# Attention masks and a bias spread over both row halves of TensorE, and a new order of blocks in a two-phase software pipeline

## The chip, the cores and the metric

One core of one Trainium2 chip runs the kernel. The metric is device time in microseconds for one launch; lower is better. The kernel before takes 3430.93 us, the median of three runs (3421.76, 3430.93 and 3432.1).

## The reference

Thirty-two independent sequences of 512 rows and 256 columns (`x`, f32) pass through four residual layers, each behind a layer norm:

1. attention A: `x + attn_a(norm(x))`, causal linear attention with 16 heads of 16, feature map `elu + 1`; a running sum of keys times values is carried along the sequence, and numerator is divided by denominator.
2. feed-forward: `x + (relu(norm(x) @ Q(W1).T + b1) @ Q(W2).T + b2)` with 1024 hidden columns; `Q` rounds the weights to -1, 0 or 1.
3. attention B: RMS-normed, rotated queries and keys, 16 query heads on 4 key heads, softmax over a causal window of 64 keys: `mask = (q >= k) & (q - k < 64)`; scores outside of the mask count as minus infinity.
4. the same feed-forward again.

The two things that the change touches in the mathematics are the mask of layer 3 and the bias `b2` of layers 2 and 4. Both are computed as before, in another way.

## The kernel before, in words

Every matrix product is made on TensorE from f32r operands that are split in a high and a low part, so most products are issued as two or three matmuls into the same PSUM bank. There are eight banks: `Q[0..3]` for the attention layers, `HID[0..1]` for the hidden columns and the norms' transposes, `Y[0..1]` for the output of the feed-forward.

**The pipeline.** The main loop runs over sequences; a pass has two phases (`phase1`, `phase2`). In phase 1 sequence `a` is in attention A, in phase 2 sequence `b` (one behind) is in attention B. Beside each attention, TensorE works on feed-forward blocks: `up(fb)` makes 128 of the 1024 hidden columns (four matmuls of 512 columns, L415), `down(fb)` adds them into `Y` (eight of 256 columns, L435). Blocks 0 to 4 (up) and 0 to 3 (down) belong to the turn that starts in this phase ("own"), the rest to the one carried over from the phase before. Between `up` and `down`, ScalarE writes the rectified block (`relu(fb)`, L948 and L949) and VectorE its low part `f_hl` (`low(fb)`, L1305). The first two passes and the last ones are written out; the loop body itself runs 29 times. One call of `phase1` and one of `phase2` make one pass.

**The order of the work is written out by hand**, as a list of block calls for each of TensorE, ScalarE and VectorE in each phase. An engine runs its list strictly in order, and semaphores order the engines among each other. So the place of a block in a list decides what waits behind it.

**Phase 1 blocks.** `qk(j)` and `values` project; `scores(ch, pair)` (L555) is eight matmuls that each use 32 rows of the array; `numer(ch, pair)` (L588, L593) uses tiles of 32 columns; `turn_numer`, `normalise`, `turn_y` (L612), `y_hi` (L1039), `y_lo` (L1437), `project` (L365) and `residual` (L1445) finish a tile of 128 rows. `qkv(t)` projects sequence `b` for phase 2; ScalarE evacuates it as `raw(t)` (L980).

**Phase 2 blocks.** GpSimd squares `raw(t)` (`squares`, L1784), VectorE sums the squares (`sums`, L1537) and makes reciprocal roots (`roots`, L1547 to L1570), then norms and rotates queries and keys (`norm_qk` L1580, `cosines` L1589, `rotate` L1595, with `sines` L1776 and L1777 on GpSimd), and `stack_hi` (ScalarE) and `stack_lo` (VectorE, L1599 and L1601) split them. `turn_qk(t, j)` (L733) transposes them; ScalarE evacuates them (`evacuate`, L1110 for queries, L1113 for keys). `scores(bl)` handles one of eight blocks of 64 queries: first `mask` (L756) writes 0 or -1e30 to two banks `Q[0]` and `Q[1]`, then four score matmuls (L761) add to them, on array rows 0 to 63 for `Q[0]` and 64 to 127 for `Q[1]`; ScalarE takes the exponentials (`exps`, L1122). `numer(bl)` (L822) follows. `own_norm` (L373) transposes the feed-forward's normed input, which `own_apply` (L1291) and `own_norm_lo` (L1297) on VectorE surround.

**The mask before** multiplies the 128-row identity, as stationary operand, with a 128-row mask that is repeated eight times along the 512 moving columns:

```python
pe.matmul(Q[g2][:, :].rearrange("p (u q) -> p u q", u=8), ident_b[:],
          kmask[:, 0 if bl else 1, :].unsqueeze(1).broadcast_to([P, 8, W]), ...)
```

`scores(bl)` issues `mask(bl, 0)` when the exponentials of the block before have left `Q[0]`, and `mask(bl, 1)` when they have left `Q[1]`.

**The bias before.** At the first `down` of a turn both `Y` banks get `b2`, by one matmul each with 64 rows (L431); both use array rows 0 to 63.

The trace takes the branch without `maxima` and `for_max` (`guarded` is false).

Of the kernel before, what the change touches and what calls it, by code (L numbers as in the profile page):

```python
# [26 lines left out]
P = 128  # L27
# [25 lines left out]
_WIDTHS = dict(ident=P, causal=P, heads=HB * HV, parity=2, kodd=W, kfirst=W, qodd=P,  # L53
# [8 lines left out]
def constants():  # L62
# [15 lines left out]
    put("kodd", np.where(odd, 0.0, MASKED))  # L78
    put("kfirst", np.where((k < W) & (k <= qq), 0.0, MASKED))
    put("qodd", np.where(np.tile(odd.T, (2, 1)), 0.0, MASKED))  # L80
    inv = (1.0 / np.float32(10000.0) ** (np.arange(0, HD, 2, dtype=np.float32) / HD)).astype(np.float32)
# [13 lines left out]
def build(nc, x, w_qkv, w_out, w_b, wo_b, gain, mix, w1, b1, w2, b2, const, out):  # L95
    with ExitStack() as ctx:
# [13 lines left out]
        kmask = sb("kmask", [P, 2, W], BF16)  # L110
        qmask = sb("qmask", [P, P], BF16)
        wqkv_h, wqkv_l = (sb(f"wqkv_{n}", [P, KB, 3 * D], F32R) for n in "hl")
# [6 lines left out]
        b2f = sb("b2f", [2 * BR, D])  # L119
        b2r = sb("b2r", [2 * BR, 2, D], F32R)  # L120
        ones_f = sb("ones_f", [P, P])
        share = sb("share", [2 * BR, P], F32R)
# [175 lines left out]
        def _(sp):  # L298
# [13 lines left out]
            sp.dma_start(b2f[:], b2.partition_broadcast(2 * BR)).then_inc(loaded, 16)  # L312
# [41 lines left out]
        def _(pe):  # L354
# [65 lines left out]
            def f_down(turn, fb, tiles=range(NT)):  # L420
# [77 lines left out]
            def program(guarded):  # L498
                def phase1(s):
# [163 lines left out]
                    scores(3, 0)  # L663
                    turn_y(1)
# [3 lines left out]
                    down(1)  # L668
                    up(3)
                    turn_numer(2)  # L670
                    scores(3, 1)
                    numer(3, 0)
                    turn_y(2)
                    next_norm(1)
# [4 lines left out]
                    up(4)  # L679
                    down(2)  # L680
                    turn_y(3)
                    qkv(s.b, 1, a + 1)
                    project(3)
                    qkv(s.b, 2, a + 1)
                    down(3)
                    qkv(s.b, 3, a + 1)

                def phase2(s):
# [182 lines left out]
                    down(7)  # L871
                    numer(0)
                    turn_qk(1, 2)
# [3 lines left out]
                    turn_numer(0)  # L877
                    scores(3)
# [50 lines left out]
        def _(act):  # L929
# [56 lines left out]
            def program(guarded):  # L986
# [91 lines left out]
                def phase2(s):  # L1078
# [63 lines left out]
                    if s.a is not None:  # L1142
                        raw(b, 2)
                        raw(b, 3)
# [700 lines left out]
```

## Time and profile before

| | us |
|---|---|
| median of three runs | 3430.93 |
| profiled execution, its time | 3421.07 |
| profiled execution, its span | 3418.4 |
| mean granted TensorE clock in it | 0.977 of full |

The profiled execution is 9.86 us faster than the median and about equal to the fastest run. Its time is 2.67 us longer than its span.
### The profile page before, as it was taken

How to read it: one execution, taken by the hardware profiler on the slowest of the kernel's cores; microseconds unless marked ns; L12 is line 12 of the kernel's file. 1: busy time of each engine (PE TensorE's matmuls, PEld its weight loads, DVE VectorE, ACT ScalarE, POOL GpSimd, SP SyncE). 2: the span in 40 equal slices, each digit the busy share in tenths (PEclk: the TensorE clock that was granted, in tenths of full speed). 3: DMA queues.
4: the chain of work that ended last, by engine and by line, in shares of the span. 5: the costliest groups of instructions: out<-in, count | busy, mean ns of one | idle time of the engine just before them, and what ended most of it. 6: DMA issues, size and time to landing. Idle time of an engine off the chain costs nothing.

```text
span 3418.4 us, 79649 instructions
## 1 busy us (share of the span) xinstructions
PE 3185.0 (93%) x27330; PEld 2446.4 (72%) x27330; DVE 2384.7 (70%) x5990; ACT 1808.4 (53%) x3585; POOL 532.1 (16%) x1164
## 2 busy tenths in 40 slices
PE   3789999999999999999999999999999999999977
PEld 2567777777777777777777777777777777777755
DVE  5567776776776677777677776677777667777654
ACT  1256555555555556555556545565555556555554
POOL 0011111111111111111111111111111111111111
PEclk9899999999999999999999999999999999999998
DMA  1000000000000000000000000000000000000000
GB/s 58 7 10 16 15 15 2 12 15 15 15 15 2 12 15 15 15 15 2 12 15 15 15 15 2 12 15 15 15 15 2 12 15 15 15 15 2 14 10 15
DMA packets 42021, 44.80 MB, mean 13 GB/s; under 512 B 2609, under 2 KB 41329, under 8 KB 41969
## 3 DMA queue, kind: packets, MB, share of 16 engines
q1 hardware_dynamic: 41968, 44.13, 4.2%
q8 instruction: 29, 0.48, 0.1%
q14 instruction: 24, 0.19, 0.0%
HBM read 21.06 MB, written 16.78 MB: 11 GB/s over the span
## 4 chain that ended last, share of the span: by engine, by line
PE 71%; issue 10%; DVE 9%; POOL 7%; ACT 2%; DVEq 0%; POOLq 0%; SPq 0%; DMA 0%; ACTq 0%
PE Q L365 11%; PE HID L415 11%; PE Y L435 11%; PE Q L555 8%; PE Q L822 4%; PE Q L593 3%; PE Q L588 3%; PE HID L373 3%; PE Q L756 3%; PE Q L761 3%; PE Q L606 2%; DVE f_hl L1305 2%; POOL ff_tmp L1739 2%; PE Q L836 2%; PE HID L733 1%
## 5 line engine op out<-in xcount | busy, mean ns | idle before, releaser
L435 PE MATMUL Y<-w2t,f_hh 128*128 128x256 f32 x2048 | 545.2, 298 | 62.1 <-DVE f_hl L1305 58.8
L435 PE MATMUL Y<-w2t,f_hl 128*128 128x256 f32 x2048 | 516.8, 285 | 0.0
L435 PEld LDWEIGHTS Y<-w2t,f_hh 128*128 128x128 f32 x2048 | 392.9, 192 | 137.0 <-DVE f_hl L1305 92.4
L948 ACT ACTIVATE f_r<-HID,b1c 128x512 f32<-128x512 f32 x512 | 350.5, 684 | 243.4 <-PE HID L415 243.4
L415 PE MATMUL HID<-ff_xh,w1t 128*128 128x512 f32 x1024 | 433.1, 423 | 19.2 <-DVE ff_xl L1297 18.9
L1305 DVE TENSOR_TENSOR f_hl<-f_r,f_hh 128x512 fp32r<-128x512 f32 x512 | 351.6, 687 | 110.6 <-ACT f_hh L949 105.1
L415 PE MATMUL HID<-ff_xl,w1t 128*128 128x512 f32 x1024 | 407.1, 398 | 0.0
L435 PEld LDWEIGHTS Y<-w2t,f_hl 128*128 128x128 f32 x2048 | 394.4, 193 | 5.9
L1407 DVE TENSOR_TENSOR a_s<-Q,cst 128x512 f32<-128x512 f32 x512 | 329.2, 685 | 89.1 <-PE Q L555 84.7
L949 ACT ACTIVATE f_hh<-HID,b1c 128x512 fp32r<-128x512 f32 x512 | 351.4, 686 | 0.0
L1039 ACT ACTIVATE a_yh<-Q 128x256 fp32r<-128x256 f32 x128 | 49.2, 385 | 496.9 <-PE Q L612 496.9
L1122 ACT ACTIVATE a_qz<-Q 128x512 f32<-128x512 f32 x512 | 278.4, 599 | 35.9 <-PE Q L761 34.8
L555 PE MATMUL Q<-a_qz,a_kT 32*128 32x256 f32 x2048 | 290.8, 401 | 2.5 <-DVE a_s L1407 2.5
L415 PEld LDWEIGHTS HID<-ff_xh,w1t 128*128 128x128 f32 x1024 | 194.1, 190 | 89.1 <-DVE ff_xl L1297 34.1
L555 PEld LDWEIGHTS Q<-a_qz,a_kT 32*128 32x128 f32 x2048 | 175.2, 184 | 56.4 <-issue 11.9
L415 PEld LDWEIGHTS HID<-ff_xl,w1t 128*128 128x128 f32 x1024 | 195.3, 191 | 26.4
L756 PE MATMUL Q<-kmask,ident_b 128*128 128x512 bf16 x512 | 166.2, 398 | 40.2 <-ACT a_qz L1122 22.6
L1784 POOL TENSOR_TENSOR a_eq<-a_s 128x320 f32<-128x320 f32 x128 | 97.8, 764 | 654.0 <-ACT a_s L980 616.1
L593 PE MATMUL Q<-a_s,a_v 128*32 128x128 f32 x4096 | 190.2, 275 | 0.5 <-DVE a_state L1417 0.5
L1757 POOL TENSOR_SCALAR at_tmp<-at_mv 128x4 f32<-128x4 f32 x64 | 12.3, 193 | 1100.2 <-DVE at_mv L1283 1100.2
L588 PE MATMUL Q<-a_qT,a_state 128*32 128x128 f32 x3072 | 159.4, 279 | 0.0
L761 PEld LDWEIGHTS Q<-b_qT,b_kT 64*128 64x128 f32 x1024 | 80.1, 194 | 107.4 <-issue 107.4
(185 smaller groups left out, 7079.1 us busy)
## 6 DMA issues: line engine op xcount, KB each, us to landing
x<-in_x SPq DMA_DIRECT2D x32, 512.0 KB, 4.3
out<-x SPq DMA_DIRECT2D x32, 512.0 KB, 3.0
b_vm<-b_v SPq DMA_DIRECT2D x64, 96.0 KB, 2.1
a_s<-in_w SPq DMA_DIRECT2D x1, 1024.0 KB, 8.1
a_qz<-in_w SPq DMA_DIRECT2D x1, 1024.0 KB, 10.5
a_s<-in_w_qkv SPq DMA_DIRECT2D x1, 768.0 KB, 4.6
cst<-in_const SPq DMA_DIRECT2D x1, 389.0 KB, 5.3
a_qT<-in_w_b SPq DMA_DIRECT2D x1, 384.0 KB, 5.8
```

Of the source, the lines that this page charges most:

```text
L365: mm = pe.matmul(dst, a, b, start=(start and k == 0 and j == 0), stop=(last and k == n - 1 and j == 2), skip_group_check=loose)
L415: mm = pe.matmul(HID[fb % 2][:], w1t[:, k, fb * P:(fb + 1) * P], src[:, k, :], start=(k == 0 and j == 0), stop=(k == KB - 1 and j == 1))
L435: mm = pe.matmul(Y[t // 2][:, (t % 2) * D:(t % 2 + 1) * D], h[:, fb % 2, t * P:(t + 1) * P], w2t[:, fb, :], start=False, stop=(fb == FB - ...
L555: mm = pe.matmul(Q[n][:, k * 2 * P:(k + 1) * 2 * P].rearrange("p (e q) -> p e q", e=2), a_kT[rows, k, ch * P:(ch + 1) * P], a_qz[rows, k, ...
L588: pe.matmul(Q[3][VW * j:VW * (j + 1), cols], a_state[:, ch - 1, k, 2 * r + e, :], a_qT[:, k, ch * P:(ch + 1) * P], start=(r == 0), stop=Fa ...
L593: mm = pe.matmul(Q[3][VW * j:VW * (j + 1), cols], a_v[:, ch, k * HB + 2 * r + e, :], a_s[:, ch % 2, r, j * P:(j + 1) * P], start=(ch == 0 ...
L756: pe.matmul(Q[g2][:, :].rearrange("p (u q) -> p u q", u=8), ident_b[:], kmask[:, 0 if bl else 1, :].unsqueeze(1).broadcast_to([P, 8, W]), ...
L948: act.activation(f_r[:, fb % 2, :], HID[fb % 2][:], ACT.Relu, bias=b1c[:, fb:fb + 1]).then_inc(f_rr, 1)
L949: act.activation(f_hh[:, fb % 2, :], HID[fb % 2][:], ACT.Relu, bias=b1c[:, fb:fb + 1]).then_inc(f_act, 1)
L1122: act.activation(b_p[:, bl % 2, g2, :], Q[g2][:, :], ACT.Exp).then_inc(b_ex, 1)
L1305: dve.tensor_tensor(f_hl[:, fb % 2, :], f_r[:, fb % 2, :], f_hh[:, fb % 2, :], ALU.subtract).then_inc(f_lo, 1)
L1407: dve.tensor_tensor(a_s[:, ch % 2, r, :].rearrange("p (h q) -> p h q", h=4), Q[r % 2][:, :].rearrange("p (h q) -> p h q", h=4), causal.uns ...
```

## The change: what it does

Three things, and no instruction of the loop is added or removed.

1. **Mask.** The two mask matmuls of a score block use 64 rows each: rows 0 to 63 for `Q[0]` and rows 64 to 127 for `Q[1]`. The roles are swapped: the transposed mask (`qmask`, which existed for the guarded branch, or the new `qfirst`) is the stationary operand, and a 64-row identity, repeated eight times, moves.
2. **Bias.** `b2r` and `share` get 128 rows; the bias of `Y[0]` uses rows 0 to 63, that of `Y[1]` rows 64 to 127.
3. **Order.** The lists of TensorE, ScalarE and VectorE are rearranged in both phases. Each list holds the same calls as before.

In the set-up, two copies of 64 columns become one of 128, and one subtraction becomes two.

```diff
                     def mask(bl, g2):
-                        pe.matmul(Q[g2][:, :].rearrange("p (u q) -> p u q", u=8), ident_b[:],
-                                  kmask[:, 0 if bl else 1, :].unsqueeze(1).broadcast_to([P, 8, W]),
+                        rows = slice(W * g2, W * g2 + W)
+                        pe.matmul(Q[g2][:, :].rearrange("p (u q) -> p u q", u=8), (qmask if bl else qfirst)[rows, :],
+                                  ident_b[rows, rows].unsqueeze(1).broadcast_to([W, 8, W]),
                                   start=True, stop=False, skip_group_check=True)
...
-                    for y in Y:
-
-                        pe.matmul(y[:], share[:], b2r[:].rearrange("p t n -> p (t n)"), start=True, stop=False,
+                    for j, y in enumerate(Y):
+
+                        rows = slice(2 * BR * j, 2 * BR * j + 2 * BR)
+                        pe.matmul(y[:], share[rows, :], b2r[rows].rearrange("p t n -> p (t n)"), start=True, stop=False,
                                   skip_group_check=True)
```

TensorE, phase 1 (start and end of the list):

```diff
                     up(5)
+                    up(6)
                     values(0)
                     qk(a, 2)
-                    up(6)
                     down(4)
+                    values(1)
                     qk(a, 3)
+                    up(7)
                     down(5)
-                    values(1)
-                    up(7)
+                    down(6)
                     turn_keys(0)
                     turn_keys(1)
-                    down(6)
                     own_norm()
...
                     scores(1, 1)
+                    turn_numer(0)
+                    up(2)
                     numer(1, 0)
-                    turn_numer(0)
                     down(0)
+                    turn_y(0)
                     scores(2, 0)
-                    turn_y(0)
-                    up(2)
                     numer(1, 1)
                     project(0)
                     scores(2, 1)
+                    numer(2, 0)
                     turn_numer(1)
-                    numer(2, 0)
                     scores(3, 0)
+                    down(1)
                     turn_y(1)
                     next_norm(0)
                     numer(2, 1)
                     project(1)
-                    down(1)
...
                     turn_numer(3)
                     up(4)
+                    turn_y(3)
                     down(2)
-                    turn_y(3)
+                    project(3)
                     qkv(s.b, 1, a + 1)
-                    project(3)
                     qkv(s.b, 2, a + 1)
+                    qkv(s.b, 3, a + 1)
                     down(3)
-                    qkv(s.b, 3, a + 1)
```

TensorE, phase 2:

```diff
                     up(5)
+                    up(6)
                     down(4)
-                    up(6)
-                    up(7)
                     down(5)
                     turn_qk(0, 0)
+                    up(7)
                     turn_qk(0, 1)
                     turn_qk(0, 2)
                     scores(0)
+                    down(6)
                     scores(1)
-                    down(6)
                     own_norm()
                     turn_qk(1, 0)
                     turn_qk(1, 1)
                     down(7)
+                    turn_qk(1, 2)
                     numer(0)
-                    turn_qk(1, 2)
                     numer(1)
                     scores(2)
                     up(0)
                     turn_numer(0)
+                    up(1)
                     scores(3)
-                    up(1)
+                    numer(2)
+                    down(0)
                     turn_y(0)
-                    down(0)
                     turn_qk(2, 0)
-                    numer(2)
                     turn_qk(2, 1)
+                    numer(3)
+                    turn_qk(2, 2)
                     project(0)
                     down(1)
-                    turn_qk(2, 2)
-                    numer(3)
                     scores(4)
...
```

Behind these, TensorE's phase 2 changes places of neighbours only. ScalarE's lists change likewise (phase 1: `relu(5)` goes ahead of `qk_exp(1)`, `qk_exp(2)` ahead of `values(0)`; phase 2: `relu(1)` and `exps(3)` go ahead of `y_hi(0)`); its phase 2 up to `exps(2)`, `relu(7)` ahead of `exps(0)` among it, stays. VectorE's ends of phase 1 and its phase 2 where they matter:

```diff
                     residual(2)
                     low(2)
                     normalise(3)
+                    low(3)
+                    y_lo(3)
                     f1_stats(2)
-                    y_lo(3)
-                    low(3)
+                    residual(3)
                     low(4)
-                    residual(3)
                     f1_stats(3)
...
                     norm_qk(2)
                     cosines(2)
-                    rotate(2)
                     norm_qk(3)
                     own_norm_lo()
-                    cosines(3)
-                    rotate(3)
+                    rotate(2)
                     finish_second(s)
...
```

VectorE's phase 2 ahead of `norm_qk(2)` (from `sums(0)` to `low(7)`) is unchanged.

## Rows read from the trace of the kernel before

**Rows 1.** The page, part 1: busy time of each engine over the span

```profile
PE 3185.0 (93%) x27330; PEld 2446.4 (72%) x27330; DVE 2384.7 (70%) x5990; ACT 1808.4 (53%) x3585; POOL 532.1 (16%) x1164
```

**Rows 2.** Stretches: two single passes, then 28 passes; column after POOL: granted clock

```profile
1788.91:1890.55 101.64, 97.77 (x855) 75.24 (x855) 73.67 (x186) 56.35 (x112) 16.61 (x36) 1.00 0.04 12
1992.28:2096.58 104.30, 101.03 (x855) 77.81 (x854) 73.69 (x186) 56.46 (x112) 16.61 (x36) 0.95 0.04 12
303.93:3171.86 2867.93, 2764.30 (x23914) 2128.61 (x23913) 2063.36 (x5209) 1578.57 (x3136) 465.14 (x1008) 0.99 0.04 12
```

**Rows 3.** Waits of TensorE in those 28 passes: total us, times, longest

```profile
PE Y L435 <- DVE f_hl L1305: 47.9, 29, 1.7
PE Q L756 <- ACT a_qz L1122: 19.2, 28, 0.7
PE Q L756 <- ACT b_kT L1113: 13.3, 28, 0.5
PE Q L733 <- ACT b_qT L1110: 8.8, 28, 0.4
PE HID L415 <- DVE ff_xl L1297: 4.0, 19, 0.2
```

**Rows 4.** Timeline of TensorE, end of phase 1 and `turn_qk(1, 0)`: start, duration

```profile
1811.09 0.28 PE L435 MATMUL Y<-w2t,f_hh 128*128 128x256 f32 x1
...
1813.36 0.39 PE L365 MATMUL Q<-wout_h,a_yh 128*128 128x256 f32 x1
...
1814.18 0.34 PE L365 MATMUL Q<-wb_h,at_xh 128*128 128x384 f32 x1
...
1815.23 0.28 PE L435 MATMUL Y<-w2t,f_hh 128*128 128x256 f32 x1
...
1831.34 0.88 PE L733 MATMUL Q<-ident_r,b_qs 128*128 128x128 f32 x8
```

**Rows 5.** Timeline of TensorE: a score block, then a bias and what follows

```profile
1837.35 0.59 PE L756 MATMUL Q<-kmask,ident_b 128*128 128x512 bf16 x2
1837.87 0.50 PE L761 MATMUL Q<-b_qT,b_kT 64*128 64x256 f32 x4
...
1788.91 0.73 PE L431 MATMUL Y<-b2r,share 64*128 64x512 f32 x2
1789.57 0.39 PE L435 MATMUL Y<-w2t,f_hh 128*128 128x256 f32 x1
1789.79 0.28 PE L435 MATMUL Y<-w2t,f_hl 128*128 128x256 f32 x1
1789.91 0.27 PE L435 MATMUL Y<-w2t,f_hh 128*128 128x256 f32 x1
```

**Rows 6.** Timeline of TensorE's weight loads around one score block

```profile
1834.64 0.11 PEld L756 LDWEIGHTS Q<-kmask,ident_b 128*128 128x128 bf16 x2 [0.46 <-issue]
1835.18 0.30 PEld L761 LDWEIGHTS Q<-b_qT,b_kT 64*128 64x128 f32 x4 [0.42 <-issue]
```

**Rows 7.** Timeline of GpSimd and ScalarE, end of phase 1

```profile
1816.50 0.72 POOL L1784 TENSOR_TENSOR a_eq<-a_s 128x320 f32<-128x320 f32 x1 [1.19 <-DVE b_ss L1537]
...
1815.43 0.44 ACT L980 ACTIVATE a_s<-Q 128x320 f32<-128x320 f32 x1 [0.98 <-PE Q L365]
```

**Rows 8.** Timeline of VectorE around that start of phase 2

```profile
1810.86 0.42 DVE L1432 TENSOR_TENSOR a_y<-Q,a_den 128x256 f32<-128x256 f32 x1
...
1815.69 0.18 DVE L1283 BATCH_NORM_AGGREGATE ff_mv<-ff_st 128x2 f32<-128x6 f32 x1 [0.16 <-DVE ff_st L1279]
1821.24 0.92 DVE L1595 TENSOR_TENSOR a_s<-a_s 128x320 f32<-128x320 f32 x1
1822.08 0.68 DVE L1305 TENSOR_TENSOR f_hl<-f_r,f_hh 128x512 fp32r<-128x512 f32 x1
1823.74 0.28 DVE L1601 TENSOR_TENSOR b_ks<-a_s,b_ks 128x128 fp32r<-128x128 f32 x1
1830.99 0.29 DVE L1601 TENSOR_TENSOR b_ks<-a_s,b_ks 128x128 fp32r<-128x128 f32 x1
```

More of the change, by code:

```diff
@@ L893, in phase2 @@
                     turn_y(1)
+                    numer(4)
                     scores(5)
-                    numer(4)
                     project(1)
@@ L900, in phase2 @@
                     next_norm(0)
+                    scores(6)
                     up(3)
+                    next_norm(1)
                     turn_numer(2)
-                    scores(6)
+                    numer(6)
+                    down(2)
                     turn_y(2)
-                    down(2)
-                    next_norm(1)
                     scores(7)
-                    numer(6)
+                    up(4)
                     project(2)
                     numer(7)
-                    up(4)
+                    qk(s.next_a, 0, b)
                     turn_numer(3)
-                    qk(s.next_a, 0, b)
+                    down(3)
                     turn_y(3)
                     qk(s.next_a, 1, b)
-                    down(3)
                     project(3)
@@ L1061, in phase1 @@
                     evacuate_numer(0)
+                    relu(1)
                     y_hi(0)
-                    relu(1)
                     evacuate_numer(1)
@@ L1066, in phase1 @@
                     y_hi(1)
+                    evacuate_numer(2)
                     next_norm(0)
-                    evacuate_numer(2)
                     y_hi(2)
@@ L1143, in phase2 @@
                         raw(b, 2)
+                    if s.a is not None:
                         raw(b, 3)
@@ L1162, in phase2 @@
                     stack_hi(2)
+                    relu(1)
+                    exps(3)
                     y_hi(0)
+                    evacuate(2, 0)
+                    evacuate(2, 1)
+                    evacuate_numer(1)
+                    evacuate(2, 2)
                     stack_hi(3)
-                    relu(1)
-                    evacuate(2, 0)
-                    exps(3)
-                    evacuate(2, 1)
-                    evacuate(2, 2)
-                    evacuate_numer(1)
                     exps(4)
@@ L1179, in phase2 @@
                     next_norm(0)
-                    relu(3)
                     exps(6)
@@ L1184, in phase2 @@
                     exps(7)
+                    relu(3)
                     evacuate_numer(3)
@@ L1213, in _ @@
                 n += 1
-            dve.tensor_tensor(b2r[BR:], b2f[BR:].unsqueeze(1).broadcast_to([BR, 2, D]), b2r[BR:], ALU.subtract).then_inc(prepared, 1)
-            n += 1
+            for low in (slice(BR, 2 * BR), slice(3 * BR, 4 * BR)):
+                dve.tensor_tensor(b2r[low], b2f[low].unsqueeze(1).broadcast_to([BR, 2, D]), b2r[low], ALU.subtract).then_inc(prepared, 1)
+                n += 1
             wo = st_wo
@@ L1486, in phase1 @@
                     next_apply()
-                    low(1)
+                    f1_stats(0)
                     y_lo(1)
                     mask(3, (0, 1))
+                    residual(1)
                     next_norm_lo(0)
-                    f1_stats(0)
-                    residual(1)
-                    f1_stats(1)
                     normalise(2)
@@ L1496, in phase1 @@
                     y_lo(2)
+                    f1_stats(1)
                     next_norm_lo(1)
@@ L1676, in phase2 @@
                         maxima(2)
-                    normalise(0)
+                    cosines(3)
                     low(0)
@@ L1680, in phase2 @@
                         maxima(3)
+                    normalise(0)
                     stack_lo(2)
-                    stack_lo(3)
+                    low(1)
+                    rotate(3)
                     y_lo(0)
-                    low(1)
                     next_stats()
@@ L1688, in phase2 @@
                         maxima(4)
+                    stack_lo(3)
                     normalise(1)
-                    next_apply()
                     y_lo(1)
@@ L1693, in phase2 @@
                         maxima(5)
+                    low(2)
+                    next_apply()
                     residual(1)
-                    low(2)
                     next_norm_lo(0)
-                    normalise(2)
                     if guarded:
                         maxima(6)
+                    normalise(2)
+                    next_norm_lo(1)
                     y_lo(2)
-                    low(3)
-                    next_norm_lo(1)
                     if guarded:
@@ L1705, in phase2 @@
                     f2_stats(0)
+                    low(3)
                     residual(2)
                     normalise(3)
-                    y_lo(3)
                     f2_stats(1)
                     f2_stats(2)
+                    y_lo(3)
                     residual(3)
```

47 lines of the change are left out of this document (23 added, 24 removed).

## The prediction, made blind

> **What bounds the kernel now.** I read the busy time first: TensorE is busy for 93% of the span, VectorE for 70%, ScalarE for 53% [rows 1]. Then the stretches of whole passes [rows 2]. A pass at the full clock takes 101.64 us. The row of 28 passes gives 2867.93 us; 28 undisturbed ones would be 2846, so falls of the clock cost 22 us in all: eight or nine of them, if each costs what this one does.
>
> Then TensorE's waits in the same 28 passes [rows 3]: 93.2 us, which is 3.3 us a pass, and all but the last row of them lie within 8 us at the start of phase 2: `down(5)` waits 1.7 us for VectorE's `low(5)`, the key transposes 0.4 us, `scores(0)` 0.5 us and `scores(1)` 0.7 us for ScalarE. Everywhere else a matmul starts as soon as the one before lets it. So for about nine tenths of a pass, time is TensorE's own work, and there a matmul saved is time saved. At the start of phase 2 it is not. There VectorE runs almost without a stop from the end of `f1_stats(3)` (1815.87) to the second `stack_lo` (1831.28), 15.4 us [rows 8], and TensorE's `turn_qk(1, 0)` begins right behind it, at 1831.34 [rows 4]. Work saved on TensorE in that stretch only makes a wait longer.
>
> **Part a: the masks.** Of a score block, the two masks and the way to the first score take 1837.87 - 1837.35 = 0.52 us [rows 5]. The four scores of 256 columns are issued as two pairs on the two row halves; their group lasts 0.50 us, and one matmul 0.28 us. With one after another at the 0.12 us at which 256 columns follow each other, four would last 0.28 + 3 x 0.12 = 0.64 us; 0.50 us is two turns. So matmuls on different row halves do run beside each other here. The two masks of 512 columns last 0.59 us, of which one is 0.38, so the second starts 0.21 to 0.22 us after the first. With 64 rows each that 0.22 us goes. Bounds: nothing (they still take turns), and 0.31 us (all of the 0.52 but one 0.21 us turn). I take 0.22, nearest to the score pairs. Eight pairs a pass, but those of `scores(0)` and `scores(1)` stand ahead of `turn_qk(1, 0)` and are worth nothing. 6 x 0.22 = **1.3 us**.
>
> **Part b: the bias.** Two matmuls on the same row half take 1789.57 - 1788.91 = 0.66 us up to the next block [rows 5]; one 512-column turn is 0.22 us. Bounds: nothing, and half of the 0.66, 0.33 us. I take 0.22, twice a pass: **0.45 us**.
>
> **Part c: changes of the array's shape.** After the bias (64 rows), the first 128-row matmul of L435 is followed after 0.22 us, the second after 0.12 us [rows 5]. I take it that a change between 128 rows, 64 rows, 32 rows and 32-column tiles costs this 0.1 us. I counted the changes in the written lists: 28 in phase 1 and 32 in phase 2 before, with each score block entering as 128-row masks and then 64-row scores; 26 and 28 after, since masks and scores now have one shape and some blocks of like shape have moved together. All six lie where TensorE doesn't wait. 6 x 0.1 = **0.6 us**. Bounds: 0 and 0.9.
>
> Weight loads bear on this part. The two mask loads begin at 1834.64, the scores' loads only at 1835.18, with 0.42 us of idle time; then four loads fit in 0.30 us, two of them on rows whose matmul has just started [rows 6]. So within one shape a load goes beside a matmul on its own rows; it is the change of shape that holds it back. The Trainium skill says otherwise (TensorE: Matmul & The Clock Gate, What overlaps and what doesn't): there a load overlaps a matmul in flight only where the row group differs. By that rule the first score loads would stay behind the masks, which adds 0.1 us for each of six blocks, and the sum below would be 19 us smaller. The rows speak against it here.
>
> **Part d: the start of phase 2.** VectorE's list is unchanged there, so the question is when it starts and whether its chain is fed. Its `rotate(0)` at 1821.24 needs `sines(0)`, which stands on GpSimd behind a root and behind `squares(2)`; that one started at 1816.50, held by the first sums, with `raw(2)` done at 1815.87 [rows 7, 8]. In the new order, counted from the end of `up(4)` (1811.1, where `down(2)` begins) [rows 4]: `normalise(3)` ends at 1811.3 [rows 8], so `turn_y(3)` now waits 0.3 us. `down(2)`, eight times 0.12 us, fills the time in which `y_hi(3)` and `y_lo(3)` (0.4 us each) follow; `project(3)` runs from 12.8 to 13.6 (0.82 us as from 1813.36 to 1814.18), behind it `qkv(1)` and `qkv(2)` (1.05 us each, as from 1814.18 to 1815.23) to 15.7, `raw(2)` (0.44 us) to 16.2; on VectorE `residual(3)`, `low(4)` and `f1_stats(3)` end at 15.5 instead of 15.87, the first sums at 16.0. `squares(2)` starts at 16.3 instead of 16.5: the chain is **0.2 us** earlier. `qkv(1)` is now behind `project(3)` and feeds `raw(1)` and `raw(2)` later, and that eats most of what the earlier `project(3)` gives.
>
> On TensorE, `up(7)` (four matmuls of 512 columns, 0.9 us) no longer stands ahead of `down(5)`, whose wait grows to about 2.1 us; `low(5)` ends at 1822.76, 0.2 us less now. `up(7)` goes between the first and second query transposes and covers the 0.4 us wait, but delays `scores(0)` by about 0.7 us: its keys are evacuated behind the second queries. On ScalarE `relu(7)` is still ahead of `exps(0)`, so the exponentials end near 1829.0. `down(6)` between `scores(0)` and `scores(1)` covers most of the 0.7 us wait for them. The walk brings `own_norm` to a few tenths earlier than before, and then `turn_qk(1, 0)` waits for `stack_lo(1)` at about 1831.1. So three waits are filled and the first is longer: idle time stays near 3.5 us, and the stretch gives only the 0.2 us of VectorE's chain. Behind it `own_norm_lo` is no longer behind `rotate(2)`, which waits for GpSimd, and `up(0)` loses its wait: 4.0 us over 28 passes, **0.15 us**. The further moves I walked through in the same way; at `numer(5)`, `turn_qk(3, 1)` and the end of phase 1 a block comes within 0.1 us of what it needs, and I charge **-0.2 us**. The moved `up` and `down` blocks cost the same 0.9 and 0.96 us in any place. DMAs are not moved.
>
> **Sum.** 1.3 + 0.45 + 0.6 + 0.2 + 0.15 - 0.2 = 2.5 us a pass. There are about 31 full passes' worth, 77.5 us, and the ends add 3.5: 81 us. The profiled execution took 3421.1, which becomes 3340. The falls of the clock I leave at nine: the idle time that precedes them keeps its size. The median of the runs stands 9.9 us above the profiled execution, as much as four more falls; I add half of it: **3345 us**.
>
> **The rivals.**
> 1. *The pairs take turns.* If masks and biases on two row halves still go one after another, parts a and b are nothing: 0.75 us a pass, 23 us, 3403. For it: a 64-row mask has its own stationary operand for each half. Against it: the score pairs. 8%.
> 2. *The gaps close and the clock stays up.* If the filled waits keep TensorE busy enough, the 22 us go as well: 3323, and a little less if the chain gets more than 0.2 us shorter. For it: the clock falls in only one pass of three, so it hangs on little. 20%.
> 3. *The new order brings waits elsewhere.* TensorE's work shrinks by 2.3 us a pass, VectorE's (73.7 us) and ScalarE's don't, and several blocks come within 0.1 us of being late. Half of the gain gone: 3380. 14%.
> 4. *Slower: the longer wait lowers the clock in every pass.* Place: the wait of `down(5)`, 2.1 instead of 1.7 us in one piece. Today a stretch at the lower level costs up to 2.7 us, since half of it falls on time in which TensorE waits anyway; the longest takes about 10 us, of which 5.1 us would be lost where it works throughout (half of it; the 10 us are worked out from the 0.95 of the clock over 104.30 us: 0.05 x 104.30 x 2). In all of 29 passes that is 148 us, less the 22 of today: 3345 + 126 = 3471. It turns the sign from 3.5 us a pass on. Against it: `up(7)` and `down(6)` now stand among the transposes and masks that follow. 6%.
> 5. *Nothing to see* (rivals 3 and 1 together): 3%.
>
> A measurement of this kernel can tell about 0.3%, 10 us, from no change. The forecast keeps 49%. Faster by over 0.3%: 49 + 8 + 20 + 14 = 91%; within: 3%; slower: 6%. The range goes from 3300 (bounds of a to c at their good end, 0.09 x 6 + 0.22 + 0.3 = 1.1 us a pass, with some falls left) to 3390 (rival 3 in full).
>
> **What would show it.** Right: the mask matmuls start 5 to 10 ns apart, with about 0.3 us from mask to score instead of 0.52; a bias pair takes 0.44 us instead of 0.66; a pass at full clock takes 99.1 us; `down(5)` waits 2 us, and TensorE's idle time stays at 3.3 to 3.7 us a pass; `up(0)` waits no more. Wrong: idle time that moved into phase 1 or behind `scores(3)` (rival 3), mask starts 0.2 us apart (rival 1), a granted clock of 0.9 or below over the 28 passes (rival 4) or of 1.00 throughout (rival 2).

## The result and the profile after

The kernel after takes **3310.99 us** (median of 4 runs, 3308.83 to 3314.02); the kernel before, run beside it on the same chip, takes 3427.22. The ratio is 0.9661, with a 95% interval of 0.9648 to 0.9674: 116 us faster, where 86 were forecast. The profiled execution has a span of 3306.9 us against 3418.4.

The page, part 1, answers to [rows 1]:

```profile
PE 3088.1 (93%) x27330; PEld 2456.8 (74%) x27330; DVE 2398.5 (73%) x5990; ACT 1788.9 (54%) x3585; POOL 545.9 (17%) x1164
```

The instructions are the same in number; TensorE is busy for 97 us less and again for 93% of the span. Four stretches of the kernel after, as in [rows 2] (three single passes, then 28; the column after POOL is the granted clock):

```profile
2231.70:2329.94 98.24, 94.55 (x859) 75.10 (x856) 74.05 (x187) 55.86 (x112) 17.06 (x36) 1.00 0.04 13
1341.59:1440.15 98.56, 95.41 (x858) 76.09 (x855) 74.14 (x187) 55.65 (x112) 17.07 (x36) 0.98 0.04 13
1242.19:1341.59 99.40, 96.28 (x858) 76.95 (x854) 74.15 (x187) 55.95 (x112) 17.06 (x36) 0.97 0.04 13
301.91:3069.63 2767.72, 2678.30 (x23917) 2137.30 (x23914) 2075.95 (x5208) 1561.88 (x3137) 477.83 (x1008) 0.98 0.04 13
```

A pass at the full clock went from 101.64 to 98.24 us, but such passes have become rare: of 27 consecutive ones, 2 in place of 19. Sixteen have a granted clock of 0.98 as in the second row and nine one of 0.97 as in the third; before, three had 0.97 and five 0.95, as the 104.30 us of [rows 2]. The falls are more and shorter. Against the median pass at the full clock (101.66 before, 98.17 after) they cost 18.6 us in 27 passes before and 17.7 after.

TensorE's waits in the same 28 passes, as in [rows 3]:

```profile
PE Y L435 <- DVE f_hl L1307: 59.8, 28, 2.1
PE Q L757 <- ACT b_kT L1114: 20.4, 28, 0.8
PE HID L372 <- DVE ff_xn L1293: 0.5, 2, 0.3
```

Five rows have become three, 93.2 us have become 80.7. `down(5)` waits 2.1 us in place of 1.7, the wait of `scores(0)` for its keys has grown from 0.5 to 0.8 us, and those of `scores(1)`, of the transposes and of `up(0)` are gone.

A score block and a bias on TensorE's timeline, as in [rows 5], and two groups of weight loads, as in [rows 6] (start, duration, tiles; "xN" is the number of instructions in a group):

```profile
2186.62 0.39 PE L757 MATMUL Q<-ident_b,qmask 64*128 64x512 bf16 x2
2186.66 0.59 PE L762 MATMUL Q<-b_qT,b_kT 64*128 64x256 f32 x4
2187.18 0.66 PE L837 MATMUL Q<-cst,a_relu 128*128 128x128 f32 x4
...
2279.64 0.50 PE L431 MATMUL Y<-b2r,share 64*128 64x512 f32 x2
2280.07 0.38 PE L435 MATMUL Y<-w2t,f_hh 128*128 128x256 f32 x1
```

```profile
2189.84 0.10 PEld L757 LDWEIGHTS Q<-ident_b,qmask 64*128 64x128 bf16 x2 [0.41 <-issue]
2189.85 0.42 PEld L762 LDWEIGHTS Q<-b_qT,b_kT 64*128 64x128 f32 x4
```

Two masks together last 0.39 us, as long as one: they run beside each other. From the first mask to the first score it is 0.04 us where it was 0.52, and from the mask to the block behind the scores 2187.18 - 2186.62 = 0.56 us. The 0.04 us is the distance of two starts and doesn't mean that the masks cost nothing: the group of four scores now lasts 0.59 us, one of them 0.28, so the second pair of scores starts 0.31 us behind the first; before it was 0.50 - 0.28 = 0.22. The scores' loads begin 0.01 us after the masks', on rows on which a mask is in flight. The bias pair takes 2280.07 - 2279.64 = 0.43 us to the next block where it was 0.66.

### The profile page after: what moved, and what is told of

Its sections match the earlier page's. It is cut to its first block, busy times and chain, and to the rows that moved or that the text cites. A ratio compares the mean times of both kernels' runs of the same rounds, so it can differ in the third digit from the quotient of the medians.

```text
span 3306.9 us, 79649 instructions
## 1 busy us (share of the span) xinstructions
PE 3088.1 (93%) x27330; PEld 2456.8 (74%) x27330; DVE 2398.5 (73%) x5990; ACT 1788.9 (54%) x3585; POOL 545.9 (17%) x1164
## 4 chain that ended last, share of the span: by engine, by line
PE 77%; issue 8%; DVE 6%; ACT 4%; POOL 4%; DMA 0%; POOLq 0%; SPq 0%; DVEq 0%; ACTq 0%
PE Q L364 14%; PE HID L414 13%; PE Y L435 13%; PE Q L555 8%; PE HID L372 4%; PE Q L823 4%; PE Q L593 3%; PE Q L588 3%; PE Q L757 2%; PE Q L606 2%; PE Q L837 2%; PE Q L733 1%; ACT a_qz L1123 1%; PE Q L762 1%; PE Q L570 1%
## 5 line engine op out<-in xcount | busy, mean ns | idle before, releaser
L414 PE MATMUL HID<-ff_xh,w1t 128*128 128x512 f32 x1024 | 448.9, 438 | 14.8 <-DVE ff_xl L1299 14.8
L414 PE MATMUL HID<-ff_xl,w1t 128*128 128x512 f32 x1024 | 419.5, 410 | 0.0
L414 PEld LDWEIGHTS HID<-ff_xl,w1t 128*128 128x128 f32 x1024 | 202.4, 198 | 28.4
L1759 POOL TENSOR_SCALAR at_tmp<-at_mv 128x4 f32<-128x4 f32 x64 | 28.2, 441 | 1073.7 <-DVE at_mv L1285 1073.7
L593 PE MATMUL Q<-a_s,a_v 128*32 128x128 f32 x4096 | 190.2, 275 | 0.0
L1034 ACT ACTIVATE a_relu<-Q 128x512 f32<-128x512 f32 x128 | 76.6, 598 | 188.5 <-PE Q L593 188.5
L762 PE MATMUL Q<-b_qT,b_kT 64*128 64x256 f32 x1024 | 158.6, 385 | 0.0
```

What stands on the lines that cost most here:

```text
L414: mm = pe.matmul(HID[fb % 2][:], w1t[:, k, fb * P:(fb + 1) * P], src[:, k, :], start=(k == 0 and j == 0), stop=(k == KB - 1 and j == 1))
L593: mm = pe.matmul(Q[3][VW * j:VW * (j + 1), cols], a_v[:, ch, k * HB + 2 * r + e, :], a_s[:, ch % 2, r, j * P:(j + 1) * P], start=(ch == 0 ...
L762: return pe.matmul(Q[g2][:, gp * REP * W:(gp + 1) * REP * W], keys(bl, g2, gp, P), b_qT[64 * g2:64 * g2 + 64, gp, bl, :], start=False, sto ...
```

## The experiments

Twelve kernels ran, each beside runs of the kernel before on the same chip. They ran in three rounds on two chips, in which the kernel before took 3425.8, 3429.1 and 3428.2 us, so medians of different rounds can be compared to about 3 us. "Pass" below is the median of the passes at the full clock, taken from 27 consecutive ones; "cost of falls" is what these 27 take beyond 27 such passes. Where no pass kept the full clock, there is no entry. A pass runs from the first `down` of one phase 1 to that of the next. Cut elsewhere, a median over one or two passes comes out up to 0.3 us higher (`low5_early` 98.49 to 98.76, `phase1_undone_sines` 98.67 to 98.87), and that of `start_undone` lies between 98.12 and 98.29; differences of 0.1 us between such rows say nothing.

| kernel | median us | ratio to before | pass | passes at full clock | cost of falls |
|---|---|---|---|---|---|
| before | 3427.22 | | 101.66 | 19 | 18.6 |
| after | 3310.99 | 0.9661 | 98.17 | 2 | 17.7 |
| masks_only | 3419.66 | 0.9982 | | 0 | |
| order_only | 3414.74 | 0.9977 | 100.51 | 2 | 44.3 |
| undo_masks | 3370.99 | 0.9842 | 100.04 | 14 | 15.5 |
| double_masks | 3340.64 | 0.9753 | 99.26 | 16 | 10.7 |
| undo_bias | 3318.45 | 0.9675 | | 0 | |
| start_undone | 3316.65 | 0.9671 | 98.26 | 15 | 19.4 |
| low5_early | 3333.77 | 0.9719 | 98.49 | 1 | 31.6 |
| sines_early | 3285.97 | 0.9586 | 97.81 | 22 | 1.8 |
| before_sines | 3423.01 | 0.9983 | 101.50 | 14 | 24.4 |
| masks_sines | 3421.52 | 0.9984 | | 0 | |
| order_sines | 3356.47 | 0.9805 | 100.04 | 21 | 6.4 |
| phase1_undone_sines | 3329.68 | 0.9711 | 98.67 | 2 | 18.8 |

### One part alone: masks_only, order_only

`masks_only` is the kernel before with the 64-row masks and nothing else; `order_only` is the kernel before with the three engines' new lists, and old masks and bias.

```diff
 masks_only, against before: mask() only
-  pe.matmul(..., ident_b[:], kmask[:, 0 if bl else 1, :]....broadcast_to([P, 8, W]), ...)
+  pe.matmul(..., (qmask if bl else qfirst)[rows, :], ident_b[rows, rows]....broadcast_to([W, 8, W]), ...)
 order_only, against before: the block lists of TensorE, ScalarE, VectorE, as in the change
```

> Order and bias as before, masks with 64 rows on both row halves. Theory A (a score block is 0.39 us shorter: 0.22 of the pair, 0.1 of the change of shape, the rest since the scores' weights load under the masks; blocks 0 and 1 hide behind VectorE's chain, and block 2 behind the wait of up(0) for the low part of the norm): 5 x 0.39 = 1.95 us a pass, an undisturbed pass of 99.7 us, about 3361 us. Theory B (only the pair's 0.22 us comes from the masks, the new order gives the rest of the result): 1.1 to 1.3 us a pass, 100.4 us, 3383. Theory C (no block hides): 8 x 0.39 = 3.1 us, 98.5 us, 3325.

> New order of all three engines, masks and bias as before. Theory A: 0.1 us of VectorE's chain, 0.2 us of the wait of up(0), four changes of shape fewer at 0.1 us: 0.7 us a pass, an undisturbed pass of 100.9 us, about 3399 us. Theory B (the order carries what the forecast missed): 1.7 us a pass, 99.9 us, 3368.

Measured: 0.9982 (0.9970 to 0.9994) and 0.9977 (0.9964 to 0.9989), so each part alone gives about 0.2% where all three together give 3.4%. None of the times put up beforehand (3325, 3361 and 3383 for the masks, 3368 and 3399 for the order) came true, since each of them left the falls as they were. Two passes of `order_only`:

```profile
2708.40:2808.91 100.51, 97.26 (x859) 75.56 (x855) 74.03 (x187) 56.30 (x112) 17.01 (x36) 1.00 0.04 12
2858.40:2960.78 102.38, 99.35 (x859) 77.19 (x855) 74.13 (x187) 56.33 (x113) 16.97 (x36) 0.97 0.04 12
```

The order is worth 101.66 - 100.51 = 1.15 us a pass, but in 23 of 27 passes the clock fell as in the second row, and in two more it fell for a shorter time. The 27 passes gain 31 us and pay 26 us more for falls (44.3 against 18.6). In `masks_only` it fell in every pass (mean granted clock 0.952). Passes at like clock can still be compared: at 0.97 before takes 103.50 us and `masks_only` 102.31, at 0.95 it is 104.30 against 102.69 (medians of 3 to 18 passes). So in the old order, too, the masks are worth 1.2 to 1.6 us a pass, and the falls hide it. The times of the parts don't add up to that of the whole, and the experiments that follow ask why.

### One part undone: undo_masks, undo_bias, double_masks

`undo_masks` is the kernel after with the 128-row masks of before; `undo_bias` has both bias matmuls on rows 0 to 63; `double_masks` issues each mask pair twice, the second time accumulating (so the mask is added twice, which leaves the output as it is).

```diff
 undo_bias, against after
-  rows = slice(2 * BR * j, 2 * BR * j + 2 * BR)
+  rows = slice(0, 2 * BR)
 double_masks, against after
   mask(bl, 1)
+  mask(bl, 0, False)
+  mask(bl, 1, False)
```

> The changed kernel with the masks of before (128 rows). Theory A: six blocks at 0.39 us come back, 2.3 us a pass, 100.5 us undisturbed, about 3383 us. Theory B: 6 x 0.22 = 1.3 us a pass, 99.4 us, 3351.

> The changed kernel with the bias of both Y banks on rows 0 to 63 again. Theory A: 0.24 us a pair comes back, twice a pass: 98.65 us undisturbed instead of 98.17, about 15 us more at the same falls of the clock, 3326 us. Theory B (a 128-row successor hides it): under 0.1 us a pass.

> The changed kernel with each pair of masks issued twice (the second pair adds 0 or -1e30 once more). If the two halves work beside each other a pair costs 0.22 us: 1.3 us more in the six blocks that count, 99.4 us undisturbed, about 3351 us. If they take turns a pair costs 0.44 us: 2.6 us more, 100.8 us, 3393. Blocks 0 and 1 cost nothing by either.

`undo_masks` costs 60 us and 100.04 - 98.17 = **1.87 us** a pass: that is what the masks are worth in the new order, between the 1.3 and 2.3 us put up for it. It lies where the prediction put it. Counted from the start of a full-clock pass, `own_norm` begins at 39.26 us in `undo_masks` and at 39.28 after: what `scores(0)` and `scores(1)` save ahead of it has all become waiting. The block behind `scores(7)` begins at 66.53 and at 64.64; each of the six score blocks between gives 0.25 to 0.41 us. `order_only` and `undo_masks` differ by the bias alone: 100.51 - 100.04 = **0.47 us** a pass. In `undo_bias` every pass had a fall and a clock of 0.98; it took 98.99 us, 0.43 more than the pass of after at the same clock (98.56), which agrees with the 0.48 us that was forecast; the time rose by 7 us and not by 15. A score block of `double_masks` on TensorE's timeline:

```profile
1508.84 0.61 PE L757 MATMUL Q<-ident_b,qmask 64*128 64x512 bf16 x4
1509.09 0.59 PE L762 MATMUL Q<-b_qT,b_kT 64*128 64x256 f32 x4
1509.61 0.39 PE L364 MATMUL Q<-wob_h,a_yh 128*128 128x256 f32 x1
```

The block takes 1509.61 - 1508.84 = 0.77 us in place of 0.56: a second pair adds 0.21 us, one turn of 512 columns and not two. The two masks of a pair don't take turns with each other, but the pair's turn isn't hidden under the scores: a second pair adds its 0.21 us in full. (Both masks on one row half would be the direct test; it was not tried. For the bias, `undo_bias` is that test.) The doubled pair adds 98.17 to 99.26 = 1.09 us a pass, for six blocks of 0.21 us, 1.3: some of it falls into waits.

### The start of phase 2: start_undone, low5_early, sines_early

Phase 2 starts with TensorE waiting for VectorE, and there the clock falls. Three edits of the kernel after, one on each engine:

```diff
 start_undone (TensorE's list, up to own_norm as before)
     up(5)
-    up(6)
     down(4)
+    up(6)
+    up(7)
     down(5)
     turn_qk(0, 0)
-    up(7)
     turn_qk(0, 1)
     turn_qk(0, 2)
     scores(0)
-    down(6)
     scores(1)
+    down(6)
 low5_early (VectorE)
     sums(2)
-    rotate(0)
     low(5)
+    rotate(0)
 sines_early (GpSimd)
-    norm_rstd(ff, first_turn(s.a))
     sines(0)
     squares(3)
+    norm_rstd(ff, first_turn(s.a))
     sines(1)
```

> The changed kernel with TensorE's list at the start of phase 2 (up to own_norm) in the order of before. Theory A (VectorE's chain sets the time at which turn_qk(1, 0) starts, in either order): an undisturbed pass stays at 98.2 us within 0.15; only the clock can move the total, by its falls, 20 us at most either way. Theory B (filling the waits with up(7) and down(6) gave part of the gain): 0.6 us a pass or more, 98.8 us undisturbed, 3330 us.

> The changed kernel with low(5) ahead of rotate(0) on VectorE, into the 0.67 us in which VectorE waits for the sines. Theory A (the pass is bound by VectorE's chain at the start of phase 2): the chain is 0.6 us shorter, 97.6 us undisturbed, 19 us less, and the wait of down(5) falls from 2.1 to 0.6 us. If the low clock follows that one long wait, up to 17 us more go: 3275. If it follows the sum of the waits, it stays: 3292. Theory B (TensorE is the bound there too): no change in the pass, 3311.

> The changed kernel with sines(0) and squares(3) ahead of the feed-forward's root on GpSimd. Theory A (rotate(0) hangs on the sines behind that root): rotate(0) starts 0.65 us earlier, the whole chain with it, 97.6 us undisturbed, about 3292 us; the root has over 5 us of slack. Theory B (the root becomes late, or the sines run slower beside VectorE): no gain or a loss of up to 1 us a pass, 3311 to 3340.

`start_undone`: TensorE's waits in 26 to 27 passes.

```profile
PE Y L435 <- DVE f_hl L1307: 32.7, 27, 1.2
PE Q L757 <- ACT a_qz L1123: 27.6, 27, 1.0
PE Q L757 <- ACT b_kT L1114: 12.9, 27, 0.5
PE Q L733 <- ACT b_qT L1111: 9.5, 27, 0.4
```

The four waits of before are back, the first at 1.2 us, and the pass takes 98.26 us, as after within what these medians can tell: theory A. TensorE's own order in this stretch moves the waiting about and gives nothing: the chain through VectorE sets it. The number of falls does hang on it (12 in place of 25), but each costs 1.6 us in place of 0.4 to 1.2, and their cost stays.

`low5_early` was to remove the longest wait. Its waits:

```profile
PE Q L733 <- DVE b_ks L1603: 55.0, 27, 2.0
PE Q L757 <- ACT b_kT L1114: 19.7, 27, 0.8
PE Y L435 <- DVE f_hl L1307: 16.1, 27, 0.6
```

`down(5)` waits only 0.6 us, but the first transpose behind it now waits 2.0 us for `stack_lo(0)`. The time is 23 us longer, outside of all that was put up for it (3275 to 3311). The timelines of GpSimd (the two halves of `sines(0)`) and of VectorE show what it met:

```profile
1778.48 0.49 POOL L1778 TENSOR_TENSOR a_s<-a_s,cst 128x160 f32<-128x160 f32 x1
1778.93 0.94 POOL L1779 TENSOR_TENSOR a_s<-a_s,cst 128x160 f32<-128x160 f32 x1
...
1778.78 0.74 DVE L1307 TENSOR_TENSOR f_hl<-f_r,f_hh 128x512 fp32r<-128x512 f32 x1
1779.98 0.92 DVE L1597 TENSOR_TENSOR a_s<-a_s 128x320 f32<-128x320 f32 x1 [0.46 <-POOL a_s L1779]
1781.88 0.69 DVE L1601 TENSOR_TENSOR b_qs<-a_s,b_qs 128x512 fp32r<-128x512 f32 x1 [0.58 <-ACT b_ks L1102]
```

The second half of `sines(0)` took 0.94 us beside `low(5)` where it takes 0.49 in the kernel after, so `rotate(0)` still waited 0.46 us, and `stack_lo(0)`, with only `sums(3)` left in front of it, waited 0.58 us for ScalarE's `stack_hi(0)`. My theory was wrong in this: `low(5)` had been filling that gap. From the last numerator matmul of phase 1 to `rotate(0)` it is 0.46 us longer than after.

`sines_early` is the fastest kernel of this study: **3285.97 us**, 0.9586 (0.9570 to 0.9602), 25 us less than after. GpSimd and VectorE in the kernel after, then in `sines_early`:

```profile
2260.98 0.32 POOL L1750 TENSOR_TENSOR ff_rstd<-ff_tmp 128x4 f32<-128x4 f32 x1
2261.26 0.49 POOL L1778 TENSOR_TENSOR a_s<-a_s,cst 128x160 f32<-128x160 f32 x1
...
2262.30 0.92 DVE L1597 TENSOR_TENSOR a_s<-a_s 128x320 f32<-128x320 f32 x1 [0.67 <-POOL a_s L1779]
```

```profile
2828.18 0.50 POOL L1778 TENSOR_TENSOR a_s<-a_s,cst 128x160 f32<-128x160 f32 x1 [2.29 <-DVE a_s L1582]
2828.64 0.75 POOL L1779 TENSOR_TENSOR a_s<-a_s,cst 128x160 f32<-128x160 f32 x1
...
2829.49 0.92 DVE L1597 TENSOR_TENSOR a_s<-a_s 128x320 f32<-128x320 f32 x1
```

In the kernel after, `sines(0)` stands behind a reciprocal root of four columns and `rotate(0)` waits 0.67 us for it; in `sines_early` the wait is gone. The chain is 0.46 us shorter: from the start of the last numerator matmul of phase 1 (L593) to that of `rotate(0)` it takes 13.01 us, against 13.47 after and 13.59 before (medians of 27 passes). A pass gains 0.36 us, 11 us over the run, and the time lies near theory A's 3292. The rest comes from the clock:

```profile
2799.35:2897.25 97.90, 94.54 (x859) 75.09 (x855) 74.26 (x187) 55.87 (x112) 17.38 (x36) 1.00 0.04 13
299.90:3042.53 2742.63, 2652.68 (x23931) 2109.95 (x23929) 2080.97 (x5211) 1564.99 (x3141) 486.70 (x1008) 1.00 0.04 13
```

Over 28 passes the granted clock rounds to 1.00 (0.98 after).

### Parts alone with the shorter chain: before_sines, masks_sines, order_sines, phase1_undone_sines

Now the same GpSimd edit is put on the kernel before, on `masks_only`, on `order_only`, and on the kernel after with the lists of phase 1 as before on all three engines.

```diff
 all four, against before, masks_only, order_only and after (the last with the old phase 1 lists)
-    norm_rstd(ff, first_turn(s.a))
     sines(0)
     squares(3)
+    norm_rstd(ff, first_turn(s.a))
     sines(1)
```

> The kernel before with one edit: GpSimd makes sines(0) and squares(3) ahead of the root of the feed-forward's norm. In the kernel after, this edit brought 25.0 us (3310.99 to 3285.97): 0.36 us a pass at full clock (98.17 to 97.81) and 16 us from falls of the clock that went away. Theory A, the edit shortens the gaps at the start of phase 2 whatever the masks and the order are: the pass at full clock goes from 101.66 to about 101.3, the falls (18.6 us in 27 passes) mostly go, time 3427 - 11 - 15 = about 3401. Theory B, whether the clock falls depends on the whole arrangement and no edit cures it by itself: the pass at full clock gets the same 0.36 us shorter, but the falls stay or grow, time 3410 to 3425.

> The kernel before with the 64-row masks alone (order and bias as before), and with sines(0) and squares(3) early. The masks alone brought 0.2% since the clock fell in every pass. Theory A, the masks are worth 1.9 us a pass and it was the clock that hid it, and this edit lifts the clock: 1.9 x 31 = 59 us less than the same kernel with 128-row masks (before_sines), about 3340, with a pass at full clock of 99.4. Theory B, without the new order the freed time becomes waiting at the start of phase 2, and the clock falls again in nearly every pass: within 15 us of masks_only less 11, 3395 to 3410.

> The kernel before with the new order alone (old masks and bias) and with sines(0) and squares(3) early. The order alone brought 0.2%, since a fall in each of 25 of 27 passes cost 44 us. Theory A: with the clock up, the order shows its 1.15 us a pass (101.66 to 100.51): 36 us less than before_sines, and a pass at full clock of 100.15, about 3365. Theory B: the falls stay, 3395 to 3405.

> The kernel after with sines(0) and squares(3) early, and with the lists of phase 1 of all three engines as before; masks, bias and the lists of phase 2 stay. It locates the order's 1.15 us a pass. Theory C, it lies mainly in phase 1, where several numerators, normalisations and feed-forward blocks changed places: a pass at full clock goes from 97.81 to about 98.8, time about 3286 + 31 = 3317. Theory D, it lies in phase 2 (fewer changes of array shape, up(0) without a wait): the pass stays within 0.2 us of 97.81, and the time within 6 us of 3286, unless the clock falls more often. Reading the two traces by phase shall tell which.

**Order.** With the clock up (21 of 27 passes), the order gives 3423.01 - 3356.47 = 67 us. Part is the pass itself, 101.50 - 100.04 = 1.46 us, 45 us over 31 passes; 18 us are falls that went away (24.4 - 6.4). Theory A of that experiment holds. That the edit cures the falls by itself does not: in `before_sines` the pass got 0.16 us shorter and 13 of 27 passes had a fall, at 24.4 us (theory B there).

**Masks.** `masks_sines` is no faster than `before_sines`: theory B in that the clock fell in each of its 27 passes, though its time, 3421.52, lies above the 3395 to 3410 put up. Waits take a smaller part. TensorE in `before_sines`, then the same blocks in `masks_sines`:

```profile
519.90 0.59 PE L756 MATMUL Q<-kmask,ident_b 128*128 128x512 bf16 x2
520.42 0.50 PE L761 MATMUL Q<-b_qT,b_kT 64*128 64x256 f32 x4
520.85 0.64 PE L822 MATMUL Q<-a_qz,b_vm 128*32 128x256 f32 x8
521.50 0.39 PE L365 MATMUL Q<-wob_h,a_yh 128*128 128x256 f32 x1
```

```profile
1342.21 0.39 PE L757 MATMUL Q<-ident_b,qmask 64*128 64x512 bf16 x2
1342.25 0.59 PE L762 MATMUL Q<-b_qT,b_kT 64*128 64x256 f32 x4
1342.77 0.64 PE L823 MATMUL Q<-a_qz,b_vm 128*32 128x256 f32 x8
1343.70 0.39 PE L364 MATMUL Q<-wob_h,a_yh 128*128 128x256 f32 x1 [0.30 <-DVE a_yl L1628]
```

The score block shrinks from 0.95 to 0.56 us, and 0.6 us later `project` waits 0.30 us for VectorE's low part: 521.50 - 519.90 = 1.60 us has become 1343.70 - 1342.21 = 1.49. The waits of 26 to 30 passes show that this happens at three kinds of block, none of which waited before [rows 3]:

```profile
PE Y L435 <- DVE f_hl L1306: 40.3, 28, 1.5
PE Q L757 <- ACT a_qz L1123: 19.5, 27, 1.0
...
PE Q L364 <- DVE a_yl L1628: 8.7, 30, 0.3
PE Q L844 <- DVE a_y L1623: 6.8, 27, 0.3
...
PE Q L837 <- ACT a_relu L1130: 5.2, 27, 0.2
```

These three are 20.7 us, 0.8 us a pass. What is left can be read where the clock is at its full level in every pass: from just ahead of the third score block to the start of the next pass. There `before_sines` takes 56.24 us and `masks_sines` 54.95, `before` 56.26 and `masks_only` 55.05 (medians of 27 passes). So in the old order the masks keep 1.2 to 1.3 us of what their six blocks save; in the new order the same stretch goes from 56.70 (`undo_masks`) to 54.72 us, 2.0. The difference is about what the three waits take: the chain numerator, divide, split, project over VectorE and ScalarE became the bound up to four times a pass. In the new order, `numer`, `turn_numer`, `turn_y` and `project` of a tile have other blocks between them, and the waits of L364, L844 and L837 aren't among those of after. That `masks_sines` isn't faster by 1.3 us a pass comes from the first part of the pass, which is 2 us longer than in the kernels with the old masks and has the low clock in every pass. Why it falls there in every pass, no run shows.

**Phase 1.** A pass of `phase1_undone_sines` at the full clock:

```profile
2942.00:3040.60 98.60, 94.55 (x855) 74.74 (x854) 73.67 (x186) 55.63 (x112) 17.80 (x36) 1.00 0.04 13
```

The median of two such is 98.67 against 97.81, so the lists of phase 1 are worth about 0.9 us: theory C. (The time is 13 us above the 3317 of that theory; 25 of the 27 passes had a fall.) But little of it lies in phase 1 itself. From the last `project` of phase 2 to that of phase 1, with the one `qkv` that the new list moves behind it (1.05 us) taken out, it is 50.08 - 1.05 = 49.03 against 48.78 us. The wait of `down(5)` shows more:

```profile
PE Y L435 <- DVE f_hl L1307: 65.1, 28, 2.4
```

That is 2.4 us where it is 1.7 in `sines_early`. With `qkv(1)` ahead of `project(3)`, as in the old list, VectorE begins its long chain later: from the last numerator matmul to `rotate(0)` it is 13.37 us, where `sines_early` takes 13.01. Phase 1's lists work in good part through the end of phase 1, where they decide when that chain starts.

## Why the prediction was right, point by point

The forecast was 3345 us in a range of 3300 to 3390, and 91% for faster; measured were 3310.99. The mechanism held. The sum was too small: between the spans of the two profiled executions lie 3418.4 - 3306.9 = 111.5 us, and it said 81. Per pass, at the full clock, 101.66 to 98.17 is 3.5 us where it said 2.5, and 1.0 us over 31 passes is the difference.

- **Part a (masks), 1.3 us: too small.** The halves run beside each other, as the score pairs said. But a block lost 0.41 us (0.97 to 0.56), not the 0.22 us of one turn: the term that was too small is "I take 0.22". The other 0.19 us came since mask and score now have one shape, so that the scores' first loads run during the masks' turn. The turn itself is still there, as in the prediction's bound of 0.31 us; the bound took the 0.45 us from the first score to the next block as fixed, and from the end of the masks' turn it is now 0.56 - 0.21 = 0.35. Against that, a mask behind a 128-row matmul starts 0.20 us after it where the 128-row mask started after 0.11: the change of shape now stands ahead of the masks, at four of the six blocks. 6 x 0.41 - 4 x 0.1 = 2.1 us, of which 1.87 arrive. TensorE's idle time in such a pass is 0.43 us longer (3.27 us in `undo_masks`, 3.70 after); `own_norm` starts at the same time in both, so 0.4 us of it is what `scores(0)` and `scores(1)` save, which the prediction rightly counted as nothing.
- **The rule weighed in part c.** The Trainium skill (TensorE: Matmul & The Clock Gate, What overlaps and what doesn't) lets a load overlap a matmul in flight only where the row group differs. The trace does not agree: the scores' loads begin 0.01 us behind the masks' on both row halves, and the first score 0.04 us behind the first mask.
- **Part b (bias), 0.45 us: right.** 0.47 by two kernels that differ in it alone; 0.43 us a pair where 0.44 was said.
- **Part c (changes of shape), 0.6 us: right in size.** `order_only` is 1.15 us faster a pass and idles 0.63 us less (3.88 to 3.25). The 0.52 us left is work, with the same instructions: the traces count 59 changes of shape a pass before, 55 in `order_only` and 53 after, six fewer in all as predicted, and the four of the order at 0.1 us would be 0.4. Not tested one by one, so the cause of the 0.52 us is argued and not shown.
- **Part d (start of phase 2), 0.2 us, and 0.15 for `up(0)`, less 0.2 for new waits: too small.** The new order took 0.63 us of idle time from a pass, where the three terms make 0.15. The chain is 0.1 us shorter up to `rotate(0)`, less than the 0.2; `down(5)` waits 2.1 us as said; `up(0)` waits no more. What failed is "So three waits are filled and the first is longer: idle time stays near 3.5 us": the filled waits shrank by more than the first grew. The 0.2 us charged for new waits isn't to be found in the waits after.
- **The falls of the clock, left at nine: wrong in number, right in cost.** 8 of 27 passes became 25, yet the stretches are shorter, and 18.6 us became 17.7. That the two agree is luck: the neighbours of this kernel run from 1.8 to 44.3 us.
- **Rivals.** The pairs do not take turns (1). The clock did not stay up (2), but in `sines_early` it nearly did (22 of 27 passes). New waits elsewhere (3) did not come after; with the masks in the old order they took 0.8 us a pass. Rival 4 had its condition, `down(5)` at 2.1 us and a fall in nearly every pass, but at 0.4 to 1.2 us each and not 5.1.
- **What was luck.** That the time lies in the range hangs in part on the cost of the falls, which happened to stay: with those of `sines_early` (1.8 us) the same passes would have made 3295 us, below it.

Outside of the 27 passes the span fell by 16.2 us (654.8 to 638.6), where the sum had 13.5 (four passes' worth at 2.5 us, and 3.5 for the ends).

## What to carry to other kernels

When a kernel alternates between a bound engine and a chain over other engines, time each part of a change both alone and undone: here masks and order gave 0.2% each, and with the bias 3.4% together. Read at one level of the clock, they don't differ so much: the masks are worth 1.2 to 1.3 us a pass in the old order and 1.9 in the new one, the order 1.2 to 1.5. Most of what each seemed to lack alone went into falls of the clock, a smaller part into waits that the new order doesn't have. Compare kernels by passes at one level of the clock and state the cost of falls beside it, or an edit of 1 us a pass can hide behind 44 us of falls. And when the bound engine waits for a chain, look at the idlest engine in it, too: 25 us came from one small GpSimd operation that stood behind another.

## What the runs showed of the hardware that I had not expected

- Where masks and scores have one shape (64 rows), the scores' loads and the first score start during the masks' turn (0.01 and 0.04 us behind the masks), and the block takes 0.56 us instead of 0.97. The turn is not hidden: another pair of masks adds 0.21 us (`double_masks`). A change of shape costs about 0.1 us: a mask starts 0.20 us behind a 128-row matmul where a 128-row one starts after 0.11.
- How many falls the clock has, and how long, changes with edits of 0.1 us a pass: from 0.98 to 0.95 in the mean of a pass, which costs 0.3 to 0.7 us (0.98), 1.0 to 1.9 us (0.97) and 2.1 to 2.6 us (0.95) over the kernels of the table. No single wait before such a stretch is longer than 2.4 us, and TensorE's idle time is 2.8 to 4.5 us a pass with and without a fall. What decides between them stays open.
- VectorE and GpSimd can slow each other: a 160-column product on GpSimd takes 0.49 us alone, 0.75 beside `cosines` and 0.94 beside `low(5)`, and the 320-column sum of `rotate(0)` takes 0.92 us where GpSimd's `squares(3)` runs beside it and 0.49 where nothing does. But not each pair does: beside `sums` (L1539) and beside the norms' low parts (L1299) the product takes 0.49 to 0.50 us, too.
